# First loop of a routed two-layer kernel: VectorE's order within a tile, and the bank that holds the head sums

## The reference

```python
up = xn @ w_up                                  # x_m, z: 256 each
conv_act = silu(x_m * conv_w[:, -1] + conv_b)
q, k, v = headwise(conv_act, q_w), headwise(conv_act, k_w), headwise(x_m, v_w)
ig = concat([q, k, v]) @ ig_w + ig_b            # 4 heads
qk = sum(q * k, per head) * 64 ** -0.5
h = (qk / (max(|qk|, exp(-ig)) + 1e-6)) * v     # per head
hn = (h - mean(h)) * rsqrt(var(h) + 1e-5) * on_w
hs = (hn + skip_w * conv_act) * silu(z)
y = x + hs @ w_down
```

## Time and profile before

| | us |
|---|---|
| time, median of 3 runs | 379.27 |
| lowest and highest run | 376.4, 379.41 |
| span of the profiled execution, first to last instruction | 411.5 |
| first loop within that span | about 65 to 237 |
| TensorE, VectorE, ScalarE, GpSimd busy | 316.7, 261.2, 168.6, 213.0 |

### The profile page before, as it was taken

How to read it: one execution, slowest core, us unless ns; L and a number is a source line. 1 busy time by engine, 2 the same in 40 slices (tenths; PEclk the granted TensorE clock), 3 DMA queues, 4 the chain that set the end, 5 groups by cost and what they waited for, 6 DMA issues and landing times.

```text
span 411.5 us, 6611 instructions
## 1 busy us (share of the span) xinstructions
PE 316.7 (77%) x1789; PEld 239.2 (58%) x1789; DVE 261.2 (63%) x876; ACT 168.6 (41%) x482; POOL 213.0 (52%) x242
## 2 busy tenths in 40 slices
PE   0929998899898888888788597868048979999920
PEld 0819865688677776777677443425025546666610
DVE  4866982796787677776888729385027456544406
ACT  2705943645354545454456204411002115566610
POOL 4998635367676666655674414237740001656530
PEclk9999999999999999999999789999659989999985
DMA  4499966024223332233354050001121000322125
GB/s 129 165 310 252 88 180 221 15 106 142 103 93 133 126 104 90 105 142 100 114 168 143 14 206 10 2 13 54 55 65 47 0 0 14 84 76 75 45 87 200
DMA packets 32883, 41.97 MB, mean 102 GB/s; under 512 B 9040, under 2 KB 24080, under 8 KB 32720
## 3 DMA queue, kind: packets, MB, share of 16 engines
q1 hardware_dynamic: 28400, 32.59, 26.9%
q0 software_dynamic: 4256, 8.74, 7.3%
q10 hardware_dynamic: 192, 0.23, 0.2%
HBM read 15.90 MB, written 10.32 MB: 64 GB/s over the span
## 4 chain that ended last, share of the span: by engine, by line
PE 28%; issue 25%; DVE 19%; POOL 17%; DMA 4%; another core or an unknown queue 3%; ACT 2%; POOLq 0%; DVEq 0%; ACTq 0%; SPq 0%
PE psum L987 8%; POOL yrows L651 7%; POOL xslots L645 6%; PE psum L1034 4%; PE psum L1007 3%; PE psum L966 2%; PE psum L1012 2%; DVE x L1402 2%; PE psum L1028 2%; DMA blocks<-yrows 2%; POOL headsum L530 2%; DVE onehot L1267 1%; PE psum L1044 1%; DVE wraw L1391 1%
## 5 line engine op out<-in xcount | busy, mean ns | idle before, releaser
L651 POOL DMA_INDIRECT yrows<-yx,blocks x31 | 29.7, 958 | 63.0 <-ACT yx L831 56.3
L620 POOL TENSOR_TENSOR rh<-c2ve,neghalf 128x8 f32<-128x8 f32 (+1 forms) x23 | 34.1, 1483 | 44.3 <-DVE c2ve L1378 41.4
L1070 PE MATMUL psum<-x1T,rec 128*128 128x512 f32 x64 | 33.2, 647 | 23.2 <-issue 17.0
L595 POOL DMA_INDIRECT xg<-xrows,gidx x39 | 39.9, 1022 | 19.2 <-issue 11.0
L606 POOL DMA_INDIRECT yrows<-yx,sidx x39 | 39.4, 1010 | 12.5 <-issue 8.6
L987 PE MATMUL psum<-yx,blocks 128*128 128x256 f32 (+1 forms) x184 | 43.4, 358 | 0.5 <-issue 0.5
L987 PE MATMUL psum<-wraw,blocks 128*128 128x256 f32 (+1 forms) x92 | 22.4, 365 | 16.6 <-DVE wraw L1391 15.0
L1070 PEld LDWEIGHTS psum<-x1T,rec 128*128 128x128 f32 x64 | 11.5, 198 | 37.5 <-issue 27.5
L805 ACT ACTIVATE xn<-psum 128x512 f32<-128x512 f32 x16 | 9.3, 596 | 55.9 <-PE psum L1070 41.8
L1114 PE MATMUL psum<-rec,yx 128*128 x62 | 31.9, 596 | 0.0
L987 PEld LDWEIGHTS psum<-yx,blocks 128*128 128x128 f32 x184 | 29.2, 191 | 2.4 <-issue 0.7
(11 more groups left out here) (221 smaller groups left out, 832.6 us busy)
## 6 DMA issues: line engine op xcount, KB each, us to landing
blocks<-rec SPq DMA_DIRECT2D x23, 523.0 KB
blocks<-yrows SPq DMA_DIRECT2D x7, 512.0 KB, 5.0
blocks<-wd SPq DMA_DIRECT2D x23, 128.0 KB
wraw<-in_L_attn_w_up SPq DMA_DIRECT2D x1, 2048.0 KB, 18.2
blocks<-xslots SPq DMA_DIRECT2D x31, 64.5 KB, 2.4
xslots<-zrow SPq DMA_DIRECT2D x1, 1984.0 KB, 19.3
x<-in_L_attn_hidden_states SPq DMA_DIRECT2D x4, 256.0 KB, 5.3
rec<-in_L_ffn_w_gate SPq DMA_DIRECT2D x1, 1024.0 KB, 17.1
```

What stands on the lines that cost most here:

```text
L595: g.indirect_dma_start(xg[:, b, h, :], None, xrows, bass.IndirectOffsetOnAxis(ap=gidx[0][:, unit(j) + h:unit(j) + h + 1], axis=0)).then_in ...
L620: g.tensor_tensor(rh[:, 0:n], c2ve[:, 0:n], neghalf[:, 0:n * NH].rearrange("p (h k) -> p h k", h=n), ALU.pow).then_inc(s_rh, 1)
L651: g.indirect_dma_start(yrows[1], bass.IndirectOffsetOnAxis(ap=xin2[:, j % R2I, D:D + 1].bitcast(U32), axis=0), yb2[:, j % R2Y, :], None).t ...
L1070: ins = t.matmul(GUd[p][g], rec2[:, e, col + c * P:col + (c + 1) * P], x1T[:, 0:DN, :].rearrange("p i t -> p (i t)"), start=True, stop=True)
```

## The change

VectorE's pass s is written in another order. Before: `prod`, `ss`, `zz`, `vs`, `nig0`, `nig`, `var`, the cell's first six operations, the next tile's `ca` chunk 0, `c2v`, `ca` chunk 1, `c2ve`, `h1`, `hs`. After: `prod`, `zz`, `ss`, `vs`, `nig0`, `nig`, `var`, `h1`, both chunks of `ca`, all eight operations of the cell, `hs`. The head sums of tile s now lie in the tile's own pair `VP[s % 2]`. TensorE's QK therefore waits for `sq` and `nig0` of the same tile, which read that pair, and V of the next tile no longer waits for the cell. No operation is added or removed.

```diff
@@ TensorE
                     at_least(pe, s_h1, s - 1)
-                    at_least(pe, s_cell, K * (s - 1) + CELL_QK)
...
                     pe.wait_ge(s_prod, s + 1)
+                    pe.wait_ge(s_sq, s + 1)
+                    pe.wait_ge(s_nig0, s + 1)
                     for h in range(halves(s)):
                         for c in range(CH):
-                            ins = t.matmul(QK[1 - b][:, h, :], prod[:, b, c, h * P:(h + 1) * P], headsum[:, c, :],
+                            ins = t.matmul(QK[b][:, h, :], prod[:, b, c, h * P:(h + 1) * P], headsum[:, c, :],
@@ VectorE: ss goes behind zz
-                if back:
-                    dve.wait_ge(s_rh, s)
-                    v.tensor_tensor(ss[:, 0:kn], cc[:, 0:kn], rh[:, 0:kn], ALU.mult).then_inc(s_ss, 1)
...
                 if back:
+                    dve.wait_ge(s_rh, s)
+                    v.tensor_tensor(ss[:, 0:kn], cc[:, 0:kn], rh[:, 0:kn], ALU.mult).then_inc(s_ss, 1)
@@ VectorE: behind var come h1, then ca, then the cell in one piece, and hs
+                if ahead:
+                    dve.wait_ge(s_thc, s + 2)
+                    at_least(dve, s_ig, s)
+                    at_least(dve, s_cask, s)
+                    for c in range(CH):
+                        ca_chunk(nb, c, halves(s + 1) * P)
```

More of the change, by code:

```diff
@@ L54 @@
 REC = IB + NH
-K, CELL_QK = 7, 5
+K = 7
 R2I, R2G, R2H, R2Y = 12, 2, 3, 4
@@ L1326, in loop1 @@
                     v.tensor_tensor(first(prod[:, b], s), first(A.rearrange("p (c t) -> p c t", c=CH), s), first(ca[:, b], s), ALU.mult).then_inc(s_prod, 1)
-                if back:
-                    dve.wait_ge(s_rh, s)
-                    v.tensor_tensor(ss[:, 0:kn], cc[:, 0:kn], rh[:, 0:kn], ALU.mult).then_inc(s_ss, 1)
-                if up:
                     dve.wait_ge(s_thz, s + 1)
@@ L1351, in loop1 @@
                         .then_inc(s_var, 1)
[L1352 to L1378, removed]
                 if back:
@@ L1385, in loop1 @@
                     ins.then_inc(s_h1, 1)
+                if ahead:
[4 more added lines that the diff above has]
+                        ca_chunk(nb, c, halves(s + 1) * P)
+                if up:
+                    dve.wait_ge(s_qk, s + 1)
+                    dve.wait_ge(s_eig, s + 1)
+                    v.scalar_tensor_tensor(negqk[:, 0:n], QK[b][:, 0:n], -1.0, eig[:, 0:n], ALU.mult, ALU.max).then_inc(s_cell, 1)
+                    dve.wait_ge(s_cell, base + 1)
+                    v.tensor_tensor(nrm[:, 0:n], negqk[:, 0:n], QK[b][:, 0:n], ALU.max).then_inc(s_cell, 1)
+                    dve.wait_ge(s_cell, base + 2)
+                    v.tensor_scalar(nrm6[:, 0:n], nrm[:, 0:n], CELL_EPS, None, ALU.add).then_inc(s_cell, 1)
+                    dve.wait_ge(s_cell, base + 3)
+                    v.reciprocal(rn[:, 0:n], nrm6[:, 0:n]).then_inc(s_cell, 1)
+                    dve.wait_ge(s_cell, base + 4)
+                    v.tensor_tensor(cc[:, 0:n], QK[b][:, 0:n], rn[:, 0:n], ALU.mult).then_inc(s_cell, 1)
+                    dve.wait_ge(s_cell, base + 5)
+                    v.tensor_tensor(c2[:, 0:n], cc[:, 0:n], cc[:, 0:n], ALU.mult).then_inc(s_cell, 1)
+                    dve.wait_ge(s_cell, base + 6)
+                    dve.wait_ge(s_var, s + 1)
+                    v.tensor_tensor(c2v[:, 0:n], var[:, 0:n * NH].rearrange("p (h k) -> p h k", h=n), c2[:, 0:n], ALU.mult).then_inc(s_cell, 1)
+                    dve.wait_ge(s_cell, base + K)
+                    v.tensor_scalar(c2ve[:, 0:n], c2v[:, 0:n], EPS, None, ALU.add).then_inc(s_c2ve, 1)
+                if back:
                     dve.wait_ge(s_h1, s)
```

## The result

| | us |
|---|---|
| before, median of 4 runs (lowest to highest) | 379.34 (376.4 to 379.86) |
| after, median of 4 runs (lowest to highest) | 391.78 (390.42 to 392.07) |
| after / before, 95% interval | 1.0354 (1.0293 to 1.0415) |
| forecast, and its range | 386.8 (376 to 390) |

The change is slower by 12.4 us, where the forecast had 7.5. The direction was right, the size was not, and the time lies 1.8 us above the range.

What follows compares the result with a forecast made beforehand. The prediction took a loop through QK, cell, `ca` and A as the bound. Added: 14 big periods x 0.21 = 2.9, 6 small x 0.67 = 4.0, end 0.6: 7.5 on 379.27 gives 386.8 us, range 376 to 390.

Steps and rivals of the forecast that it cites:

- The reading of the late ends: TensorE's QK and second-layer down products announced late, 33.2 us of VectorE waits, belong to the profiled execution; timed runs have almost none.
- The ring that the forecast named for the kernel before: Big tile's loop QK, cell, `ca`, A, V, IG, PC, VT, QK, said to set the period at 7.07 us.
- the first piece of the ring of a big tile: From `c2ve` to `ss` through GpSimd's `rh`, 1.97 us of the new 7.28 us loop through cell and `ca`.
- The small tiles: Same loop through GpSimd in small tiles: 5.36 us against 4.69, 0.67 longer each, 4.0 us for six.
- The end of the loop: Last tile: two half-size `h1` operations now ahead of the cell, on the path to the last scatter, about 0.6 us.
- TensorE's ring of 7.1 to 7.2: TensorE's loop in a big tile after the change, A to the next A, claimed to stay under 7.28 us.
- QK's wait: QK behind `sq` and `nig0` starts 0.25 us later in a big tile, claimed to cost nothing by itself.
- "Faster": Rival: late announced ends are a fixed delay in every run, so the change gains, about 373 us; chance 0.15, restated 0.14.
- "Same": Rival: TensorE's instruction rate or another limit near 7.3 us already holds big tiles; about 381 us; chance 0.2, restated 0.25.
- That A would still wait for `ca`: Rival in TensorE's tile loop: product A still stands for the activations after the change; given no chance of its own.

Runs made afterwards that it cites:

- the last edits: Kernel before with V's halves each waiting for their own `h1` chunk (ratio 0.9993), with `zz` moved behind `nig` (0.9932), and with both (0.9818).

## Why the direction was right and the size wrong

**Where the time went.** The two undisturbed traces, of before (span 374.8) and of after (390.3), can be summed by the starts of `c2ve`: to the first one 74.76 and 76.33, +1.57; the fifteen periods of big tiles 106.12 and 113.92, +7.80; the one from the last big to the first small tile 5.75 and 6.93, +1.18; the six small ones 29.21 and 34.09, +4.88; from the last to the end of the span 158.96 and 159.03, +0.07. Together 15.5. Of the first 1.57, 0.59 lie ahead of the first tile, where the two kernels do the same (the first `yx` starts at 64.60 and 65.19), and 0.98 in it. The medians differ by 12.4; before's own runs go from 376.4 to 379.9, and the one with this trace took 376.5. Part of that spread goes with the clock: on the chip of this trace, four runs of before with a mean granted clock of 0.968 or 0.969 took 375.67 to 376.84, two with 0.963 and 0.964 took 377.8 and 378.49, and one with 0.930 took 388.18.

**The reading of the late ends held.** They were absent in every later trace, with 7.09 and 4.70 us of before where the forecast had worked out 7.07 and 4.69. What made one execution announce them late stays open. The ring that the forecast named for the kernel before (QK, cell, `ca`, A) did not bind it, though: in the undisturbed tile the first chunk of `ca` has ended when the second begins, at 116.70, and A begins at 117.00, behind Z. With the 0.15 that A takes to start, that ring had some 0.15 to spare (estimate), and what set the 7.09 were the two other rings that the last edits found. That 7.07 came so near is partly luck.

**The step that failed** is the first piece of the ring of a big tile, "`rh` itself 1.68". The 1.68 was read from a tile in which `h1` stood beside the start of `rh`. The change puts `hs` there, which reads both operands from SBUF, and `rh` came out at 2.05 in fifteen tiles and at 1.16 in place of 1.04 in small ones: 15 x 0.37 + 6 x 0.11 = 6.2 us of the 8.0 by which the forecast falls short of the two traces (7.4 without the 0.59 ahead of the first tile, 4.9 by the medians). Two forms of `hs` hold `rh` alike, a shift of `hs` by 0.15 shifts the end of `rh` as far, and with `hs` elsewhere `rh` takes 1.68 and the ratio falls from 1.0354 (1.0439 in the second measurement) to 1.0249.

The Trainium skill states the rule that was missed: "SBUF — State Buffer", section "SBUF: two separate sides", says that VectorE and GpSimd share one pair of SBUF ports as a lock, that a VectorE operation with two inputs in SBUF takes it against a GpSimd operation that reads SBUF, and that the later one blocks. The rows agree where `hs` comes first. The page also has a GpSimd operation that starts first keep the pair to its end. The rows differ: in the undisturbed trace of before `hs` begins 0.73 into `rh` and takes its 0.69 all the same, so the measurement decides that `rh` does not hold the pair that long; in the small tile of the run with a delay, 0.20 was enough.

**Smaller errors.** `ss` was thought to wait some 0.1 for `rh`; it waited 0.38. There are 15 big periods and not 14, and the first tile (+0.98) and the one where the sizes change (+1.18) were left out. The small tiles were sized well: 5.50 us where the clock holds against 5.36 forecast. The end of the loop, priced at 0.6, came out at 0.07 behind the last `c2ve`, and the last small period, without a `ca`, grew by 0.38 and not 0.67. TensorE's ring of 7.1 to 7.2 stayed below, as said, and QK's wait costs nothing in the new order: the run with `rh` short has the same waits of TensorE, and its big tiles take 7.16.

**A term that no step had** is the granted clock. In small tiles of the after trace it falls, and one tile takes 6.53 us in place of 5.50, while the trace of before has 0.97 from 205 to 215 us, where its small tiles end. The windows of after (us, busy time of each engine and number of instructions, then the granted clock):

```profile
205.00:215.00 10.00, 9.40 (x58) 8.54 (x58) 8.40 (x39) 5.94 (x18) 6.39 (x7) 0.83 0.44 141
215.00:230.00 15.00, 11.36 (x63) 10.29 (x63) 11.21 (x49) 6.32 (x20) 5.90 (x6) 0.77 0.13 45
```

In the run with `hs` in another form, whose tiles are otherwise those of after, it falls in an early big tile too, which then takes 9.91 us: VT has waited 1.09 us for `vs`, and behind that QK takes 1.77 us in place of 1.03 at half clock (0.50, so 1.2 GHz).

```profile
87.00:89.00 2.00, 2.00 (x11) 1.90 (x11) 1.49 (x4) 1.92 (x5) 0.96 (x1) 0.50 0.15 43
```

```profile
86.77 1.07 PE L1027 MATMUL psum<-ident,vs 128*128 128x128 f32 x4 [1.09 <-DVE vs L1338]
87.63 1.77 PE L1035 MATMUL psum<-headsum,wraw 128*128 128x4 f32 x8
```

The kernel after has the same wait there and keeps the full clock in its first trace:

```profile
87.00:89.00 2.00, 1.86 (x15) 1.65 (x16) 1.49 (x4) 1.94 (x5) 1.11 (x2) 1.00 0.10 33
```

In its second trace the same wait of 1.08 us is followed by a QK of 1.84 us, and this is the tile of 9.99. So a wait of TensorE may or may not bring the clock down; what decides it stays open. The undisturbed trace of before has no such wait in that stretch and keeps 1.00.

**The rivals.** "Faster" had its condition refuted by the second profile of before. "Same" asked for a limit near 7.3 that holds the old order; there is none, 7.09 was two rings of the same length, and shortening both gave 6.80. That A would still wait for `ca` did not happen.

## What to carry to other kernels

A duration belongs to its neighbours: when a move puts another operation beside a step on the critical ring, take that step's duration from a place with the same neighbour, and where GpSimd is on the ring, ask which VectorE operation with both operands in SBUF runs when it is issued. Sum a loop's period round every ring, and look for a second one of nearly the same length before spending an edit on the first: here neither of two edits moved the big tiles alone, and both together took 0.29 us off each. Where a profiled span is much longer than the timed runs, profile again before trusting its waits.

## What the runs showed of the hardware

A GpSimd operation of 8 values a partition, issued while VectorE reads two operands from SBUF, waits for that operation's end: the power ends 1.54 us behind it, with `hs` in either form, and the product 0.06 us. The power of 4 values, in the small tiles of after, ends 0.91 behind it. Each is 0.13 or 0.14 less than what the operation takes alone (1.68, 0.20 and 1.04), with overlaps of 0.25 to 0.65 us (0.65 with the delay ahead of `hs`, 0.25 in the small tiles). `h1`, with one operand in PSUM, left the power at 1.68 where it ran when the power started. `hs` that begins after `rh` leaves both durations as they are, if it begins late enough: 0.20 behind did in the one tile that has it. Where it begins 0.02 behind, in a small tile of the run with `zz` alone moved, `rh` takes 1.34 in place of 1.04:

```profile
194.55 1.34 POOL L620 TENSOR_TENSOR rh<-c2ve,neghalf 128x4 f32<-128x4 f32 x1
194.57 0.45 DVE L1387 TENSOR_TENSOR x1T<-h,wraw 128x256 f32<-128x256 f32 x1
```
